# A three-layer interaction network on one Trainium2 core: units of 4 values of d and 32 rows in place of 8 values of d and 16 rows

## The reference, cut to what matters

```
hidden = x                                   # x: 512 rows b, 39 fields, 32 values of d, float32
for i in range(3):                           # W0: (39*39, 200), W1 and W2: (100*39, 200)
    z = einsum('bmd,bnd->bmnd', x, hidden).reshape(B, -1, D)
    cur = relu(einsum('bcd,co->bod', z, W[i]) + b[i][None, :, None])
    if i < 2: hidden, direct = cur[:, :100, :], cur[:, 100:, :]
    else:     direct = cur
    finals.append(direct)
return sum(concatenate(finals, axis=1), axis=-1)     # over d: (512, 400)
```

## Time and profile before

| | |
|---|---|
| median of three runs | 2799.02 us |
| the profiled execution | 2799.83 us |
| its span, first to last instruction | 2798.1 us |
| TensorE busy, matmuls | 2707.5 us, 97% |
| VectorE busy | 2722.4 us, 97% |
| ScalarE busy | 1763.7 us, 63% |
| DMA packets, and their share of 16 engines | 346786, 47.7% |
| mean granted TensorE clock | 0.997 |

### The profile page before, as it was taken

One profiled execution on the slowest core, in us unless ns is written; L12 is line 12 of the kernel. 1 busy time (PEld: TensorE's weight loads), 2 busy tenths in 40 slices (PEclk: granted clock), 3 DMA queues, 4 the chain that ended last, 5 costly groups with the idle time before them and its releaser, 6 DMA issues.

```text
span 2798.1 us, 56046 instructions
## 1 busy us (share of the span) xinstructions
PE 2707.5 (97%) x18112; PEld 2642.5 (94%) x18112; DVE 2722.4 (97%) x3090; ACT 1763.7 (63%) x3178; POOL 1.2 (0%) x11
## 2 busy tenths in 40 slices
PE   1799999999999999999999999999999999999998
PEld 1799999999999999999999999999999999999998
DVE  3899999999999999999999999999999999999997
ACT  2566666666666666666666666666666666666664
POOL 0000000000000000000000000000000000000000
PEclk9999999999999999999999999999999999999999
DMA  8454544454454454454454454454454445444441
GB/s 193 110 126 109 129 123 108 118 134 108 123 129 109 112 138 110 117 131 112 109 138 114 113 130 117 108 132 120 108 128 121 111 122 129 109 117 124 119 112 54
DMA packets 346786, 333.97 MB, mean 119 GB/s; under 512 B 151970, under 2 KB 281614, under 8 KB 346638
## 3 DMA queue, kind: packets, MB, share of 16 engines
q1 hardware_dynamic: 346762, 333.67, 47.7%
HBM read 332.73 MB, written 8.37 MB: 122 GB/s over the span
## 4 chain that ended last, share of the span: by engine, by line
PE 93%; DMA 3%; DVE 1%; ACT 1%; SPq 1%; issue 1%; ACTq 0%; DVEq 0%
PE acc L620 63%; PE acc L621 28%; DMA xb<-x_by_unit 1%; PE summed L638 1%; PE turned L632 1%; DMA xb<-in_L_rec_b_dram 1%; ACT z_high L495 0%; DMA w_rows_again<-in_L_rec_W_dram 0%; DVE z_low L354 0%; DMA xb<-in_L_rec_W_dram 0%; DVE w_split L327 0%; ACT w_split L523 0%; ACT hid L514 0%; DVE z L350 0%; SPq L170 0%
## 5 line engine op out<-in xcount | busy, mean ns | idle before, releaser
L620 PE MATMUL acc<-w_split,z_high 128*128 128x400 f32 (+1 forms) x8832 | 2656.2, 368 | 71.8 <-DVE z_low L354 64.7
L621 PE MATMUL acc<-w_split,z_low 128*128 128x200 f32 (+1 forms) x8832 | 2252.9, 255 | 0.0
L620 PEld LDWEIGHTS acc<-w_split,z_high 128*128 128x128 f32 (+1 forms) x8832 | 1662.2, 188 | 119.8 <-issue 86.2
L495 ACT ACTIVATE z_high<-z 128x1024 fp32r<-128x1024 f32 (+2 forms) x1152 | 1181.9, 1026 | 898.1 <-DVE z L350 812.6
L621 PEld LDWEIGHTS acc<-w_split,z_low 128*128 128x128 f32 (+1 forms) x8832 | 1691.4, 192 | 0.0
L354 DVE TENSOR_TENSOR z_low<-z,z_high 128x1024 fp32r<-128x1024 f32 (+2 forms) x1152 | 1373.2, 1192 | 7.7 <-ACT z_high L495 7.0
L350 DVE TENSOR_TENSOR z<-hid,xb 128x1024 f32<-128x1024 f32 (+1 forms) x1024 | 1232.2, 1203 | 8.4 <-ACT hid L514 5.4
L514 ACT ACTIVATE hid<-turned 32x128 f32<-32x128 f32 x768 | 205.3, 267 | 8.9
L511 ACT ACTIVATE hid<-turned 96x512 f32<-96x512 f32 x256 | 150.1, 586 | 35.1 <-PE turned L632 33.3
L361 DVE TENSOR_TENSOR s<-acc,half 128x200 f32<-128x200 f32 x384 | 144.6, 377 | 9.8 <-ACT half L500 9.8
L339 DVE TENSOR_TENSOR z<-x_left,x_right 118x896 f32<-118x896 f32 x128 | 140.2, 1096 | 0.0
(11 more groups left out here) (21 smaller groups left out, 35.9 us busy)
## 6 DMA issues: line engine op xcount, KB each, us to landing
xb<-x_by_unit SPq DMA_DIRECT2D x384, 384.0 KB, 4.3
x_right<-x_by_unit SPq DMA_DIRECT2D x384, 136.5 KB
xb<-x_by_unit SPq DMA_DIRECT2D x384, 128.0 KB, 4.9
xb<-x_by_unit SPq DMA_DIRECT2D x128, 336.0 KB
xb<-x_by_unit SPq DMA_DIRECT2D x128, 84.0 KB
x_left<-x_by_unit SPq DMA_DIRECT2D x384, 19.5 KB
xb<-in_L_rec_W_dram SPq DMA_DIRECT2D x6, 600.0 KB, 8.6
x_by_unit<-in_r_x_dram SPq DMA_DIRECT2D x128, 19.5 KB
```

The lines of the kernel that those rows point to most:

```text
L495: nc.scalar.activation(z_high[slot][0:rows, 0:n * T], z[slot][0:rows, 0:n * T], ACT.Copy).then_inc(high, 1)
L620: nc.tensor.matmul(a[:, 0:2 * O], z_high[slot][0:rows, tok], w, start=(c == 0), stop=False, skip_group_check=True)
L621: last = nc.tensor.matmul(a[:, 0:O], z_low[slot][0:rows, tok], w[:, 0:O], start=False, stop=(c == chunks - 1), skip_group_check=True)
```

## The change

PARTS = 8 takes the place of QUARTERS = 4. A unit still has 128 tokens, but of 4 values of d of 32 rows: STEPS = 4, BT = 32. Eight units make a group and there are 16 groups. The running sum of the direct half goes over eight units, and the matmul over d, ScalarE's copy and the sending are done once per eight units. The runs that `turn_x` reads have 4 floats. `group_b` has 32 columns. The straight code at both ends has eight units instead of four, and the loop has 14 passes of eight periods instead of 30 passes of four. Layer 0 is summed and sent when j == PARTS - 2.

```
-QUARTERS = 4
-STEPS = D // QUARTERS
+PARTS = 8
+STEPS = D // PARTS
...
-                if j == 2 and layer0:
+                if j == PARTS - 2:
                     send(0, m)
...
                 if turn:
-                    turn_x(m + 1, j)
+                    turn_x(m + (j + 4) // PARTS, (j + 4) % PARTS)
...
-            for j in range(1, QUARTERS):
+            for j in range(1, PARTS):
                 period(0, j)
-            with sp.Fori(0, UNITS // QUARTERS - 2) as i:
-                for j in range(QUARTERS):
+            with sp.Fori(0, UNITS // PARTS - 2) as i:
+                for j in range(PARTS):
                     period(i + 1, j)
...
             def directs(l, rows, q):
 
-                u = rows * QUARTERS + q
+                u = rows * PARTS + q
...
-                if j == 2:
+                if j == PARTS - 2:
                     sum_over_d(0, m)
```

More of the change, by code:

```diff
@@ L162, in turn_x @@
                 dst = [[T, F], [STEPS, BT], [1, STEPS]]
-                to, at = rows * (QUARTERS * XROWS * T) + q * (XROWS * T), rows * (BT * F * D) + q * STEPS
+                to, at = rows * (PARTS * XROWS * T) + q * (XROWS * T), rows * (BT * F * D) + q * STEPS
                 sp.dma_start(bass.AP(xt_t, to, dst), bass.AP(x, at, src)).then_inc(xt_done, 16)
@@ L244, in _ @@
             sp.wait_ge(xt_done, 128)
-            turn_x(1, 0)
+            turn_x(0, 4)
             sp.wait_ge(product, 2)
@@ L258, in period @@
             def period(m, j, layer0=True, pairs=True, turn=True, ahead=True):
-                n, par = m * QUARTERS + j, j % 2
+                n, par = m * PARTS + j, j % 2
                 at = first(n)
@@ L283, in _ @@
             load_pairs(3)
-            for j in range(1, QUARTERS):
+            for j in range(1, PARTS):
                 period(0, j)
-            with sp.Fori(0, UNITS // QUARTERS - 2) as i:
-                for j in range(QUARTERS):
+            with sp.Fori(0, UNITS // PARTS - 2) as i:
+                for j in range(PARTS):
                     period(i + 1, j)
[L289 to L294, removed]
+            last = UNITS // PARTS - 1
+            for j in range(PARTS):
+                to_come = PARTS - 1 - j
+                period(last, j, layer0=to_come >= 2, pairs=to_come >= 3, turn=to_come >= 4, ahead=to_come >= 1)
             send(1, last)
@@ L297, in _ @@
             for l in range(3):
-                sp.wait_ge(o_out[l], 16 * (UNITS // QUARTERS + 1))
+                sp.wait_ge(o_out[l], 16 * (UNITS // PARTS + 1))
         @block.gpsimd
@@ L467, in _ @@
             period(0, 1, first(1), first(1) % RING, before2=False, last_low=False)
[L468 to L476, removed]
+            for j in range(2, PARTS):
+                period(0, j, first(j), first(j) % RING)
+            with dve.Fori(0, UNITS // PARTS - 2) as i:
+                for j in range(PARTS):
+                    period(i + 1, j, first(i * PARTS + (PARTS + j)), first(j + PARTS) % RING)
+            last = UNITS // PARTS - 1
+            for j in range(PARTS):
+                n = last * PARTS + j
+                period(last, j, first(n), first(n) % RING, layer0=j < PARTS - 2, before0=j < PARTS - 1)
             at = first(UNITS)
@@ L483, in _ @@
                 lows(at + g - 1, slot_of(at + g - 1), P, group_chunks(g - 1))
-            directs(2, last, 2)
+            directs(2, last, PARTS - 2)
             lows(at + 3, slot_of(at + 3), P, group_chunks(3))
             sums(2, UNITS - 1)
-            directs(2, last, 3)
+            directs(2, last, PARTS - 1)
         @block.scalar
@@ L590, in _ @@
             period(0, 1, first(1), first(1) % RING, before2=False)
[L591 to L599, removed]
+            for j in range(2, PARTS):
+                period(0, j, first(j), first(j) % RING)
+            with act.Fori(0, UNITS // PARTS - 2) as i:
+                for j in range(PARTS):
+                    period(i + 1, j, first(i * PARTS + (PARTS + j)), first(j + PARTS) % RING)
+            last = UNITS // PARTS - 1
+            for j in range(PARTS):
+                n = last * PARTS + j
+                period(last, j, first(n), first(n) % RING, layer0=j < PARTS - 2, before0=j < PARTS - 1)
             at = first(UNITS)
@@ L634, in sum_over_d @@
             def sum_over_d(l, rows):
-                pe.wait_ge(direct_in[l], rows * QUARTERS + QUARTERS)
+                pe.wait_ge(direct_in[l], rows * PARTS + PARTS)
                 if not (isinstance(rows, int) and rows == 0):
@@ L655, in period @@
             def period(m, j, base, sl, layer0=True, before0=True, before2=True):
-                n = m * QUARTERS + j
+                n = m * PARTS + j
                 def slot(p):
@@ L689, in _ @@
             period(0, 1, first(1), first(1) % RING, before2=False)
[L690 to L698, removed]
+            for j in range(2, PARTS):
+                period(0, j, first(j), first(j) % RING)
+            with pe.Fori(0, UNITS // PARTS - 2) as i:
+                for j in range(PARTS):
+                    period(i + 1, j, first(i * PARTS + (PARTS + j)), first(j + PARTS) % RING)
+            last = UNITS // PARTS - 1
+            for j in range(PARTS):
+                n = last * PARTS + j
+                period(last, j, first(n), first(n) % RING, layer0=j < PARTS - 2, before0=j < PARTS - 1)
             sum_over_d(1, last)
```

6 lines of the change are left out of this document (3 added, 3 removed).

## The result

The changed kernel took 3005.09 us (median of four runs, 3001.94 to 3013.09), the kernel before on the same chip 2799.14 us (2798.72 to 2800.57): ratio 1.074, 95% interval 1.0727 to 1.0753. The forecast was 2818 us, and the range ended at 2840. Slower was right; 206 us against 19 was not. The profiled execution took 3013.09 us, its span is 3011.4 us.

A forecast was written before the change was run, and what follows sets the result against it. VectorE was taken to bound the kernel. From the median of 2799.02 us, +3.8 (adds) - 2.4 - 1.0 (stalls) + 2.5 - 1.0 (start) + 17 (jumps) = +18.9 us gave 2818 us, range 2797 to 2840.

The forecast's parts named there:

- What bounds the kernel: Steady part: VectorE, busy 841.65 of 842 us, sets the pace; TensorE waits for VectorE, VectorE for almost nobody.
- Sums over d: Matmuls over d on TensorE: 48 of 96 go, sparing it 21 us, hidden by VectorE's stream; counted as 0.
- The rival that 21 us come through: TensorE is the bound after all, so its spared time counts: about 2780 us; chance 0.05.
- Running sum and stalls once a group: VectorE: +3.8 us for writes that become adds; -2.4 and -1.0 us for half of its once-a-group stalls.
- The loop: Backward jumps: doubled code is not held, each of 13 jumps stalls VectorE 1.3 us for a fetch: +17 us, 0 to 34.
- cover of 1.7 us: VectorE at a jump back: queued work hides 2.2 us less about 0.5 us of a 3.0 us code fetch.
- Turning x: Copy of x in 16-byte runs: twice the packets, twice the time, hidden in the steady part: 0 there.
- At the start: First turnings delay weight loads: +2.5 us; VectorE's wait behind layer 0's first send moves to the full pipeline: -1.0 us.
- The costly reads: Rival: a turning of x takes over 8 us and delays the next unit's loads; some 3000 us at 10 us; chance 0.04.

## Why the prediction was wrong

*What bounds the kernel*: right, and closer than it said. VectorE's starts add up to the unit's time, taking a write off it shortened two units of four and the kernel by up to 7 us, and taking half of the sums off TensorE shortened nothing. But TensorE stands right behind, some 0.1 us a unit behind by the estimate above, where the prediction took it to have room.

*Sums over d*: 0, right. The rival that 21 us come through falls: straight code with 32-byte reads took 2799.68 us, not 2780.

*Running sum and stalls once a group*: +3.8 - 2.4 - 1.0 = 0.4 us; with neither jumps nor short reads the changed kernel is 0.9 us over the one before, within an interval of 2.8 us either way. The cause of the stall was misread, though. Laid on the sum and the sending of layer 0, it should have gone to j = 6; in the straight kernel with 32-byte reads it is still at j = 2 (the first two rows, 1.18 us from the product to the low part) and not at j = 6 (the last two, 1.00). That it comes once a group held; what makes it stays open.

```profile
1475.48 1.10 DVE L348 TENSOR_TENSOR z<-hid,xb 128x896 f32<-128x896 f32 x1
1476.66 1.23 DVE L352 TENSOR_TENSOR z_low<-z,z_high 128x1024 fp32r<-128x1024 f32 x1
...
1559.89 1.08 DVE L348 TENSOR_TENSOR z<-hid,xb 128x896 f32<-128x896 f32 x1
1560.89 1.22 DVE L352 TENSOR_TENSOR z_low<-z,z_high 128x1024 fp32r<-128x1024 f32 x1
```

*The loop*: the mechanism was right, the price was the step that failed. "VectorE stalls 3.0 - 1.7 = 1.3 us a jump, 13 jumps: 17 us", at most 34. Alone, jumps cost 91 us. The fetch was priced by the landing of a send (3.0 us), but takes 3.6 to 3.8 us on TensorE and over 4 us on VectorE, whose cover of 1.7 us was about right (4.1 - 2.2 = 1.9): a row of data said too little of a fetch of code. And "TensorE and ScalarE stall at the same jumps ...; I add nothing for them" was wrong twice: eight periods on TensorE alone cost 2.9 us a jump, which add to VectorE's, and after the first piece it needs a second, which no term had. VectorE's lateness covers TensorE's first fetch nearly whole in the changed kernel (0.55 us are left in the jump shown), but not the second.

*Turning x*: "If twice the packets take twice the time" failed: 5.4 us, 3.3 times. In the steady part the idle stretch still covers it, as the prediction had it, except where loads are tight (20 us by the traces). At the start, +1.5 us in the sum, it costs 28 to 29 us. What stands behind the first turnings was bounded by "one more turning's time" each, 1.65 us, the doubled time again, and SP's issue was left at 0.9 us; the second turning's issue begins 7 us late and takes 7.0 us.

*The costly reads* were given 0.04, with the price set at over 8 us a turning. The rival's place, the next loads of x, was not where it hurt. For the most part it was TensorE's second fetch: 60 us that neither the jump nor the reads cost alone, 45 of which went when the loop's start was moved. No case of the prediction has it, so that the rival's "some 3000 us" came near the result is luck.

By the experiments the 206 us are 91 (jumps), 55 (reads) and 60 (both). The page of the Trainium skill (Runtime: NRT & Kernel Launch, Instruction fetch mechanics) gives TensorE's store 128 KiB. The traces agree so far: 80 KB of TensorE's code are held, and the code of eight periods, for which each pass brings 12 pieces of 16 KB anew, is not. Its window of two pages does not hold for TensorE's five pieces, which go round without a fetch.

## What to carry to other kernels

Before a loop's body is doubled, count each engine's instructions in it and compare the pieces with what the trace shows to be held; here, past what was held, every jump back cost the engines a fetch each, and these added up. Straight code cost nothing here (2799.68 us). When a layout change makes the runs of a copy in DRAM shorter, price it by more than its packets, and look at what else must get through while they fly: a fetch of code is one such thing.

## What the runs showed of the hardware that was not expected

- A copy from DRAM to DRAM in runs of 16 bytes took 5.4 us for 1888 packets, in runs of 32 bytes 1.6 us for 944: 2.9 ns a packet against 1.7 (medians of all turnings), so the packet itself became dearer.
- One turning's packets kept a fetch of 16 KB of code waiting to about their end: at 13 jumps of 13 it came 5.7 to 7.7 us behind the branch, with the turning later or of 32-byte runs 4.0 to 5.1 us. In the stretch shown 17.7% of the DMA engines' time was in use.
- After stands of TensorE of 3.8 and 4.4 us the granted clock was 0.60 and 0.61 in the next 4.3 and 5.5 us; a matmul of 128x400 took 0.58 us in part of them, where 0.36 us is usual, so each stand costs more than its length.
- GpSimd's max took from 1.1 us (128x100, near 1456 us) to 9.2 us (128x200, near 1443 us) beside a busy VectorE, by the profile's rough times, and VectorE's full products took up to 1.56 us from start to start instead of 1.135.
